# First score operands from head-repeated weights, with all placement tables of the schedule rewritten

## What is computed

```python
mod = (silu(c) @ wmod)...                       # sa, ca, ga, sb, cb, gb for each batch
h = layernorm(x) * (1 + ca) + sa
x = x + ga * attention(h)                       # 16 heads of 16, softmax(q k^T / 4) v, then wo
h = layernorm(x) * (1 + cb) + sb
x = x + gb * moe(h)                             # 2 shared and 16 routed experts of width 128, top 4 gates
```

## Time and profile before

| | |
|---|---|
| median of 3 runs | 959.78 us (956.91 to 961.59) |
| the profiled execution | 961.51 us, its span 959.7 us |
| PE busy | 880.8 us (92%) |
| ACT busy | 655.2 us (68%) |
| DVE busy | 637.9 us (66%) |
| POOL busy | 380.8 us (40%) |
| DMA | 78.28 MB, mean 82 GB/s |

### The profile page before, as it was taken

One profiled execution on the slowest core, in us unless ns is written; L12 is line 12 of the kernel. 1 busy time (PEld: TensorE's weight loads), 2 busy tenths in 40 slices (PEclk: granted clock), 3 DMA queues, 4 the chain that ended last, 5 costly groups with the idle time before them and its releaser, 6 DMA issues.

```text
span 959.7 us, 15806 instructions
## 1 busy us (share of the span) xinstructions
PE 880.8 (92%) x5928; PEld 427.1 (45%) x5928; DVE 637.9 (66%) x1239; ACT 655.2 (68%) x1109; POOL 380.8 (40%) x323
## 2 busy tenths in 40 slices
PE   5668788999999989999899998999999999998897
PEld 3222233255444444445444463445544554446565
DVE  6764776667778747877478765877577667824442
ACT  4178785677876867758687676768787767772542
POOL 4422143234525343424433344353433423455363
PEclk9759798999999999999999998999999999999999
DMA  7502301620315014230245003262014210221140
GB/s 250 175 25 93 93 1 41 181 73 2 89 44 189 1 61 121 78 107 1 61 122 159 24 24 104 69 176 88 29 39 127 107 44 2 89 100 44 47 159 23
DMA packets 48876, 78.28 MB, mean 82 GB/s; under 512 B 6680, under 2 KB 43032, under 8 KB 44704
## 3 DMA queue, kind: packets, MB, share of 16 engines
q1 hardware_dynamic: 48800, 77.27, 25.9%
HBM read 64.25 MB, written 12.86 MB: 80 GB/s over the span
## 4 chain that ended last, share of the span: by engine, by line
PE 67%; DVE 12%; ACT 9%; POOL 5%; issue 4%; DMA 2%; SPq 0%; POOLq 0%; ACTq 0%; DVEq 0%
PE scalar_bank L844 18%; PE down_bank L982 17%; PE vector_bank L912 11%; PE scalar_bank L895 6%; PE vector_bank L895 6%; DVE neg_max L801 5%; PE vector_bank L844 3%; DMA gates<-gates_by_expert 2%; DVE rows L681 2%; ACT probs L636 2%; ACT f_ring L602 2%; PE scalar_bank L924 2%; ACT q_aug L625 1%; PE vector_bank L930 1%; ACT gelu L664 1%
## 5 line engine op out<-in xcount | busy, mean ns | idle before, releaser
L801 DVE TENSOR_REDUCE neg_max<-vector_bank 128x1 f16<-128x512 f32 x479 | 306.0, 686 | 72.6 <-PE vector_bank L895 60.8
L636 ACT ACTIVATE probs<-scalar_bank 128x512 f32<-128x512 f32 x483 | 261.0, 602 | 109.9 <-PE scalar_bank L895 100.4
L586 POOL TENSOR_TENSOR act_lo<-gelu,act_hi 128x512 f16<-128x512 f32 x144 | 176.7, 1247 | 245.3 <-ACT act_hi L616 241.1
L788 DVE TENSOR_TENSOR gelu<-gelu,gates 128x512 f32<-128x512 f32 x128 | 112.5, 894 | 113.1 <-ACT gelu L664 92.2
L982 PE MATMUL down_bank<-down_hi,act_hi 128*128 128x256 f16 x576 | 160.1, 278 | 1.3 <-POOL act_lo L586 1.3
L982 PE MATMUL down_bank<-down_hi,act_lo 128*128 128x256 f16 x576 | 157.7, 274 | 0.0
L982 PE MATMUL down_bank<-down_lo,act_hi 128*128 128x256 f16 x576 | 157.7, 274 | 0.0
L664 ACT ACTIVATE gelu<-scalar_bank 128x512 f32<-128x512 f32 x144 | 84.7, 597 | 76.8 <-PE scalar_bank L844 55.5
L895 PE MATMUL scalar_bank<-q_aug,k_aug 64*128 64x512 f16 x483 | 118.7, 394 | 15.1 <-ACT gelu L664 12.6
L895 PE MATMUL vector_bank<-k_aug,q_aug 64*128 64x512 f16 x479 | 116.5, 404 | 12.8 <-ACT q_aug L625 6.0
L912 PE MATMUL vector_bank<-probs,v_aug 128*32 128x512 f32 x992 | 125.3, 628 | 0.0
(11 more groups left out here) (167 smaller groups left out, 1206.8 us busy)
## 6 DMA issues: line engine op xcount, KB each, us to landing
gates<-gates_by_expert SPq DMA_DIRECT2D x32, 1024.0 KB, 4.9
q_aug<-q_parts SPq DMA_DIRECT2D x96, 64.0 KB, 3.5
k_aug<-k_parts SPq DMA_DIRECT2D x96, 64.0 KB, 2.5
x_pre<-in_x SPq DMA_DIRECT2D x8, 512.0 KB, 4.0
x_post<-in_x SPq DMA_DIRECT2D x8, 512.0 KB, 5.1
out<-x_post SPq DMA_DIRECT2D x16, 256.0 KB, 2.5
gates<-in_w_up SPq DMA_DIRECT2D x4, 576.0 KB, 11.7
gates<-in_w_down SPq DMA_DIRECT2D x4, 576.0 KB, 4.3
```

Of the source, the lines that this page charges most:

```text
L586: pool.tensor_tensor(act[1][:, c, :], gelu[:, n % NGELU, :], act[0][:, c, :], ALU.subtract).then_inc(s_elo, 1)
L636: scalar.activation(probs[:, n % U, :], src[:], ACT.Exp, scale=SCALE).then_inc(taken[kind], 1)
L788: dve.tensor_tensor(g, g, gates[:, (n - NSH) % 8, :], ALU.mult).then_inc(s_gated, 1)
L801: dve.tensor_reduce(neg_max[:, (u // 2) % TT, at:at + 1], src[:], AX.X, ALU.max, negate=True).then_inc(done, 1)
```

## The change

The change has two parts.

**The start.** For batch 0 the operands of heads 0 to 7 don't go through DRAM. ACT and DVE write `wide`, the q and k weights of these heads with each head's 16 columns repeated four times (`four_times`, `first_heads`); the product of `wide` with h then has each head's q or k in the four row blocks at once. There are eight such products, the new items `first` (a pair of heads times q or k). ACT evicts each twice, with scales and biases (`pick`, `shift`) that are zero or one by row block, and POOL combines the two into `q_aug` or `k_aug`. `pick` and `shift` are made by ten small DVE instructions, a spread identity (`ident_wide`) and four tiny matmuls. Two 128x2048 fills of the second operand set go from DVE to POOL, behind its `power(0, ...)`. The rest of the modulations, the gates' mods and the router split come in a new item `late` on PE and DVE. `qk`, `qk_out`, `qk_in` 0 and 1 and `no_max` of batch 0 are gone; `qk` 2 and 3 stay.

**The tables.** `BESIDE`, `MOVED`, `HEAD`, `LEAD` and all place tables are written anew: the four full tables become one with even spacing, `MOVED` keeps six entries (all of batch 1), and the items of batch 0's start get places in `EARLY`.

```diff
-R_KINDS = ("warm", "exp", "onT", "h1T", "qk", "h2T", "up")
+R_KINDS = ("warm", "first", "exp", "onT", "h1T", "qk", "h2T", "up")
+SKIPPED = {"qk": 2}
...
+    ("qk", 0): (-4, 14.9), ("qk", 1): (-3, 3.2), ("qk", 2): (-3, 15.2), ("qk", 3): (-2, 3.2),
+    ("v", 0): (-1, 5.9), ("v", 1): (-1, 9.9),
+    ("oT", 0): (4, 3.2), ("oT", 1): (4, 5.2), ("oT", 2): (4, 5.9), ("oT", 3): (4, 7.2),
+    ("onT", 0): (4, 9.2), ("onT", 1): (4, 9.9), ("wo", 0): (4, 13.9), ("wo", 1): (4, 16),
+    ("stats2", 0): (4, 18), ("rows2", 0): (4, 20), ("h2T", 0): (5, 5.2), ("h2T", 1): (5, 7.2),
+    ("logit", 0): (5, 11.2), ("top8", 0): (5, 13.2), ("idx8", 0): (5, 13.9), ("hit", 0): (5, 15.2), ("chosen", 0): (5, 16),
+    ("e16", 0): (6, 0), ("esum", 0): (6, 1.2), ("einv", 0): (6, 1.9), ("gates", 0): (6, 3.2), ("gateT", 0): (6, 5.9),
+    ("qk_out", 0): (-4, 16), ("qk_out", 1): (-3, 3.9), ("no_max", 0): (-3, 4.2), ("qk_in", 0): (-3, 5.2), ("qk_in", 1): (-3, 7.9),
+    ("qk_out", 2): (-2, 0), ("qk_out", 3): (-2, 5.2), ("qk_in", 2): (-2, 6), ("qk_in", 3): (-2, 11.2),
+    ("gates_out", 0): (6, 7.2), ("gates_in", 0): (6, 7.9), ("gates_in", 1): (6, 9.2), ("gates_in", 2): (7, 18), ("gates_in", 3): (8, 18),
...
+HEAD = [("x_pre", 0, 1), ("h1T", 0, 0), ("h1T", 1, 0), ("late", 0, 0), ("first", 0, 0), ("first", 1, 0), ("first", 2, 0), ("first", 3, 0)]
+EARLY = {("first", 4): 4, ("first", 5): 5, ("first", 6): 8, ("first", 7): 9,
+         ("qk", 2): 12, ("qk_out", 2): 12.1, ("qk", 3): 14, ("qk_out", 3): 14.1, ("qk_in", 2): 15, ("qk_in", 3): 16,
+         ("v", 0): 18, ("v", 1): 19, ("wsplit", 0): 23, ("wsplit", 1): 24, ("wsplit", 2): 25, ("mods", 0): 26,
+         ("stage", 3): 27, ("stage", 4): 28, ("stage", 5): 29}
-LEAD = {"light": (12, 4, 6), "full": (0, 0, 2)}
+LEAD = {"first": (12, 2, 8), "light": (12, 2, 8), "full": (0, 0, 2)}
+EVEN = [1 + 2 * k for k in range(8)]
+FULL = {"max": EVEN, "exp": [k + .5 for k in EVEN], "down": [.5 + 3.2 * k for k in range(5)], "up": [16.5 + k for k in range(5)],
+        "gated": [17.6, 18.6, 19.6, 20.6, 24.1], "hi": [17.61, 18.61, 19.61, 20.61, 24.11], "turn": [18], "early": [24, 26, 27, 28],
+        "pv": [24.5, 25.5, 26.5, 27.5], "ahead": [25.4, 26.4, 27.4, 28.4], "oraw": [28.9]}
+PLACES = [dict(FULL), dict(FULL), dict(FULL), dict(FULL), LIGHTLY, AFTER, OPENING]
...
             power(0, mv[0], rstd[0], s_ln1, s_rs1)
+            pool.memset(q_aug[1][:].bitcast(U32), 0).then_inc(s_aug1, 1)
+            pool.memset(k_aug[1][:].bitcast(U32), 0x3C003C00).then_inc(s_aug1, 1)
...
+                elif kind == "first":
+                    pair, w = divmod(n, 2)
+                    wait(pool, taken[kind], PER[kind], b, n + 1)
+                    pool.tensor_tensor((q_aug, k_aug)[w][0][:, pair, :], f_ring[:, F_RING[item][0], :], act[0][:, n % SETLEN, :],
+                                       ALU.add).then_inc(s_first, 1)
...
+                elif kind == "first":
+                    if n == 0:
+                        pe.wait_ge(s_wide[0], 4)
+                        pe.wait_ge(s_wide[1], 4)
+                        pe.wait_ge(s_h1lo, 2)
+                    pair, w = divmod(n, 2)
+                    split_product(dst[:], [([p[:, DC * w + c, P * pair:P * (pair + 1)] for p in wide], [p[:, c, :] for p in h1])
+                                           for c in range(DC)]).then_inc(sig, 1)
```

More of the change, by code:

```diff
@@ L53 @@
 PER = {"max": 64, "maxT": 4, "exp": 64, "oT": 4, "onT": 2, "wo": 2, "v": 2, "logit": 1, "gateT": 1,
-       "h1T": 2, "qk": 4, "h2T": 2, "up": NEX, "pv": 16, "down": NEX * TT}
+       "h1T": 2, "first": 8, "qk": 4, "h2T": 2, "up": NEX, "pv": 16, "down": NEX * TT}
 FIRST, LIGHT = -1, 6
-BESIDE = {("stats1", 0): (-6, 14.77), ("rows1", 0): (-5, 6.46), ("x_pre", 0): (-6, 0.91), ("h1T", 0): (-4, 0.1),
[4 rows of a table removed]
[L63 to L70, removed]
@@ L109 @@
-LEAD = {"light": (12, 4, 6), "full": (0, 0, 2)}
-MOST = {"max": [0, 1.19, 2.34, 5.19, 7.34, 9.19, 11.43, 12.79], "exp": [2.61, 4.46, 6.46, 8.46, 10.46, 12.51, 14.46,
-    15.81], "down": [0.5, 3.7, 6.81, 10.14, 14.05], "up": [16.13, 17.43, 18.33, 20.23, 22.69], "gated": [17.23, 18.11,
-    20.28, 23.33, 25.03], "hi": [17.6, 18.52, 21.9, 24.94, 29.53], "turn": [17.18], "early": [22.03, 29.41, 29.41,
-    29.41], "pv": [24.75, 24.84, 25.2, 25.54], "ahead": [22.25, 22.45, 22.86, 25.83], "oraw": [27.21]}
@@ L134 @@
+LIGHTLY = {**FULL, "max": [1, 3, 5, 7, 9, 11, 13, 15], "turn": [3]}
+AFTER = {**FULL, "down": [1 + 4.4 * k for k in range(5)], "up": [3 + 4.4 * k for k in range(5)],
+         "gated": [7.4 + 4.4 * k for k in range(5)], "hi": [7.41 + 4.4 * k for k in range(5)]}
+OPENING = {**LIGHTLY, "early": [19, 20.5, 22, 23.5, 24.5, 25.5, 27, 28.5]}
 TURN_BY_SCALAR = (0, 1)
-PLACES = [MOST, SECOND, THIRD, LAST, LIGHTLY, AFTER]
+PLACES = [dict(FULL), dict(FULL), dict(FULL), dict(FULL), LIGHTLY, AFTER, OPENING]
@@ L217, in plan @@
             g, place = MOVED.get((kind, n, b), (at + 4 * b, usual))
-            if (kind, n, b) not in HEAD and not (kind in ("x_pre", "stats1", "rows1") and b == 0):
-                put(g, place, (kind, n, b))
+            if b > 0 or kind not in ("x_pre", "stats1", "rows1", "h1T", "qk", "qk_out", "qk_in", "no_max", "v"):
+                if (kind, n, b) not in HEAD:
+                    put(g, place, (kind, n, b))
+    for (kind, n), place in EARLY.items():
+        put(FIRST, place, (kind, n, 0))
     for n, (g, place) in enumerate(SPLITS):
@@ L235, in ring @@
         values = kinds is V_KINDS and item[0] == "pv" and item[1] % TT == 0
-        if lent and item == ("max", 0, 0):
+        if lent and item == ("v", 1, 0):
             order.insert(0, banks)
@@ L357, in heads_of, with four_times, first_heads @@
             return row[:, 0:H * VW].rearrange("p (h w) -> p h w", h=H)[:, :, 1:VW]
-        def qk_part(part, n, b):
-            return act[part][:, n, :] if b == 0 and n >= 2 else qk[part][:, n % 2, :]
+        def four_times(row):
+            return row.rearrange("p (h r d) -> p h r d", r=4, d=DH)
+        def first_heads(weights):
+            return weights[:, 0:P].rearrange("p (h d) -> p h d", d=DH).unsqueeze(2).broadcast_to([P, 8, 4, DH])
         def piece(parts, n):
@@ L880, in _ @@
                         pe.matmul(bank(item)[:], ident16[:], w4[0][:, 0, :, :].rearrange("p c d -> p (c d)"), start=True, stop=True)
+                if kind == "late":
+                    pe.wait_ge(s_rep, 1)
+                    pe.wait_ge(s_small, 64)
+                    for pair in range(4):
+                        ins = pe.matmul(DB[1][:, 2 * pair:2 * pair + 2], ident_wide[:, P * pair:P * (pair + 1)], bqk[:, 0:4:2], start=True, stop=True)
+                    ins.then_inc(s_pickT, 1)
+                    pe.wait_ge(s_mod0, 2)
+                    modulations(1)
+                    pe.wait_ge(s_pick, 9)
+                    modulations(2)
                 if kind not in PER:
```

192 lines of the change are left out of this document (97 added, 95 removed), and 18 rows, old and new, of tables (BESIDE, MOVED).

## The result

The changed kernel takes 1005.0 us (median of 4 runs, 1002.6 to 1005.5) against 958.4 for the kernel before in the same session (4 runs, 953.0 to 961.6): ratio 1.049, 95% interval [1.043, 1.054]. It is 46.6 us slower (45 against the 959.9 us that the kernel before takes in the next session), where 16 us less was forecast.

A forecast was written before the change was run, and what follows sets the result against it. PE, busy 92%, was taken to bound the kernel, so gains must shorten its waits or slow stretches. From 961.5: -21.6 queue, +6 spacing, +2 tail, -4 start gives 943.9, stated as 944; the forecast's own range is 928 to 955.

The forecast's parts named there:

- The queue: SP's order in the full batches: `qk_out` 0 behind its product ends DVE's three waits for the gates' DMA, -21.6 us.
- Even spacing: Full groups' tables: dependent items stand closer, +6 us over six batches (0 to +16); the tail +2 more.
- The two distances: `onT` 1 to `wo` 0 and `h2T` 1 to `logit`, each now 4 places: 0.5 us each, 1.0 a batch.
- stays ahead of both in the even order: Full groups: PE needs 1.6 us per two places, DVE about 1.3, ACT a little less, so PE stays ahead.
- Rival A: Group ends: a late gate multiplication delays ACT, PE lacks banks for exps; 1.25 us a group, +32, 976 us; chance 0.28.
- Rival B: SP's loads ahead of `gates_out` make first gates 3 us late in six batches, 18 given back, 962 us; chance 0.12.
- D: Queue repair: only the -11.3 of the groups themselves comes back, 954 us; chance 0.08.
- C: Start loses, block whole and ACT late: +3 for -4, 951 us, or 957 with spacing at 12; chance 0.10.
- Light groups: The light groups keep their work: 0 us, one chain of 3.4 either way.
- The start: Batch 0's start: first maximum 6 to 8 us earlier, gain for DVE's stream -4 us (bounds -8 and +3).
- comes as much earlier: Start: the first exp, 55.14 before, moves earlier as much as DVE's stream gains, to near 51.
- if ACT keeps up: Condition on the earlier first exp: ACT must keep up with eight pairs of evictions in place of two.

The follow-up runs named there:

- the best kernel: The kernel before with one entry changed, the store of q (`qk_out` 0) moved behind its product: 942.8 us, ratio 0.982.

## Why the prediction was wrong

The runs give a ledger from the kernel before to the changed one. Each step is one edit, in this order:

| step | time | difference |
|---|---|---|
| before (its runs beside the next row's) | 959.9 | |
| store of q behind its product | 942.8 | -17.1 |
| new start | 954.4 | +11.7 |
| new light and tail tables, lead | 955.3 | +0.9 |
| new places beside the groups, `rows2` excepted | 965.5 | +10.2 |
| `rows2` from 25.08 to 20 | 992.4 | +26.9 |
| one even table in place of four | 1005.0 | +12.6 |

The last steps depend on their order. `rows2` costs 26.9 here, 20.3 in the best kernel, and together with `hit` and `chosen` only 13.2 under the even table (1005.0 against 991.8). The even table costs 12.6 here, 23.9 where the three places are late (991.8 against 967.9), and 37.7 where all places beside are old (993.0 against 955.3). So no share of the 50 belongs to either alone. Both lose at the same place, the end of group 4b and the start of 4b + 1, and either hides much of the other. They don't do it by the same wait: with the even table alone, ACT waits less for its gate multiplication there (0.88) than in the best kernel (1.07).

**The queue (-21.6, bound -11.3): right, and a little large.** Alone it gave 17, between the two. The three waits are gone in every kernel that has it: the longest left on the gates' DMA in any of them is 2.4 us.

**The places beside the groups (no term): a step that failed, since it wasn't there.** Alone they cost 37.1, of which `rows2` is 26.9. The part on the even spacing compared distances (`onT` to `wo`, `h2T` to `logit`) and let it rest at that. `rows2` moved by five places, past gate multiplications, and I didn't cost it, though the diff had it in plain sight. Its place needs two looks: it waits for POOL, which in turn stands for DVE's statistics; and behind it on DVE stand the multiplications on which ACT and, through the table load and exps, PE depend. The sum would have been 1.91 of waiting and 1.38 of work, 3.3 on DVE; measured are 2.8 on ACT (3.85 - 1.07) and 4.6 on PE in group 17, the slow clock included.

**Even spacing (+6, bound +16): the other step that failed.** The two distances that made up the whole term cost nothing (1006.1 with them undone). The even full table itself costs 12.6 to 37.7. What I had wrong is the sentence that PE "stays ahead of both in the even order": PE's idle time in the groups 16 and 17 rises from 0.8 to 4.3 us with the table alone (windows above). With `rows2` late (991.8, 993.0) the waits are spread: ACT waits 0.4 to 1.4 for a gate multiplication in every group, and ACT's four copies of the turn (2.39 us) stand ahead of the last two gelus of group 16 and PE waits 0.90 for them. In the best kernel the copies stand there too and PE has no such wait. No run moved the turn, the ups or the copies alone, so what the even table costs is placed, and its cause stays open.

**Rival A (976, +32): nearer than my forecast.** It said: DVE late with one gate multiplication, ACT late by it, PE without a bank for the exps. That is the chain of the timelines above, but it was `rows2` that set it off. The signs came: periods over 110, and a wait of ACT's in every full group, 16 times in four batches, though PE's own waits for ACT's gelus and exps came only 8 and 8 times there. Its +32 for the even table is near the 37.7 of that table alone. That is luck as far as is known: I priced it at 1.25 us in each of 26 groups, from an imagined delay of one 0.65 us multiplication, while 6.5 of the 7.5 us that it costs a batch (113.8 against 106.3) sit in two groups. My argument against it, that an old table had its ups just as close, looked at PE's items and not at DVE's. Even A was too low for the whole, since the moved `rows2` was in neither.

**Rival B (the block moves to `gates_in` 0): didn't happen.** What is left of the waits for the gates is 2.9 us in four, 1.8 of it in group 6. Nor was it D, the half gain: 17 of the 21.6 came, and were spent. C, a losing start, was right in sign, and the +3 it gave the start was too small by 9.

**Light groups (0): wrong, about +8.** Of the +10.2 above, 8.7 lie before the first gate rows (194.62 against 185.92), in groups 3 and 4. No run told which item it is.

**The start (-4): right up to the first maximum, wrong behind it, +12.** Forecast for the first scores 31.7 to 34.1, measured 32.25, and the first maximum at 32.67, though by terms that cancelled. The small DVE instructions cost 1.3 (10.85 - 9.56; I took 2), POOL's fills blocked DVE for 3.20 (4.58 - 1.38; I took 2) and the modulations cost 7.1 in place of 3.5; the products took 6.2 (25.88 to 32.03) in place of 7.8, and scores began 0.22 behind them, where I had allowed 2.4. Modulations and products traded places here: whichever comes first on PE runs at the slow step (see the last section), so that part of the 3.6 us which the modulations lost came back in the products. The Trainium skill, page "SBUF — State Buffer", section "Who interferes with whom", has this exclusion as a lock for the whole instruction, which the prediction put at 3.6; the trace agrees in the main (3.20 of the 3.6), and with the fills moved the rows take 1.38 again and the run is 4.2 shorter. Then I wrote that the first exp "comes as much earlier", near 51. It came at 64.23. The step that failed is the condition attached to it, "if ACT keeps up": ACT stood idle for 3.38, 3.34 and 2.84 us just before, and PE had four products of the first heads, two more of `qk` and v (by the rows, 24 matmuls of `first`, 12 of `qk` and those of v) ahead of the first exp tile. I had counted the instructions up to the first maximum and none between it and the first exp. Behind that stood the SP queue: the same kind of mistake as the earlier trace rows showed in the steady stage, two items (the modulations' store and the weight load) behind loads that wait for a product.

## What to carry to other kernels

When a schedule is rewritten, go through every item that changes its order against others on its engine, not through those whose distance shrank. For each ask what it waits for and who is waiting behind it; a cheap item that waits, put ahead of a producer for the critical engine, cost 20 to 27 us here (13 with two others where the even table had already spent most of it), and nothing in the shares of busy time showed it.

When repairs of single parts each give little and the loss stays, undo them in pairs before looking for further causes. Two causes that lose time at the same place hide one another: here 37 us each alone, 50 together.

An early result is worth only what the next queues let through. In the new start each wait removed uncovered the next one, twice on the same SP queue; list all that stands between the early result and its last consumer, on every queue, before counting the gain.

## What was not expected of the hardware

A PE gap of about 1.5 us (busy 1.22 of 2.70) was followed, 1.4 us later, by some 3 us at the 1.2 GHz level in group 17: the products step 0.43 apart there (505.82, 506.25, 506.67), against 0.21 to 0.22 elsewhere. The same gap in group 13 was followed by products 0.22 apart at a granted clock of 1.00. So such a gap can bring the lower clock and need not, and its price, 1.4 us a time here, can't be counted on either way. Of the 4.6 us that early `rows2` costs group 17, the idle part is 2.1.

In the start the products between 25.88 and 27.55 also step 0.42 apart, and the 24 modulation matmuls before them take twice their time of before, though the window from 22 to 27 shows a granted clock of 1.00. That 1.00 is not a measurement: the first clock record of this trace lies at 27.52, just where the step falls to 0.22. The kernel before shows the same at 21.37, its first record: 0.43 until then, 0.22 after. Before the first record the duration and step of the rows tell the clock, and the window's column doesn't.
